# Cross attention's scores in two fp32r passes on split operands, with the pieces of the round laid out anew

## The reference

```python
q = _split_heads(query @ q_w + q_b, B)          # 16 heads of 16
k = _split_heads(key @ k_w + k_b, B)
v = _split_heads(value @ v_w + v_b, B)
scores = jnp.einsum('bhqd,bhkd->bhqk', q, k) * SCALE
attn = jax.nn.softmax(scores, axis=-1)
out = jnp.einsum('bhqk,bhkd->bhqd', attn, v)
return out.transpose(0, 2, 1, 3).reshape(B, -1, EMBED_DIM) @ o_w + o_b
...
x = _layernorm(x + _L0_xattn_ref(x, ctx_1024, ctx_1024, ...))
logits = x @ gate_w
w, sel = jax.lax.top_k(softmax(logits), 2)      # two of eight experts, beside two shared ones
```

## Time and profile before

| | |
|---|---|
| median of 3 runs | 971.75 us (963.71 to 973.4) |
| the profiled execution | 971.51 us, span 969.7 us |
| PE matmul busy | 863.9 us, 89% of the span |
| PE weight loads | 648.7 us, 67% |
| DVE | 607.3 us, 63% |
| ACT | 451.7 us, 47% |
| POOL | 344.7 us, 36% |
| chain that ended last | PE 56%, DVE 15%, ACT 10%, DMA 6%, POOL 5% |

### The profile page before, as it was taken

How to read it: one execution, slowest core, us unless ns; L and a number is a source line. 1 busy time by engine, 2 the same in 40 slices (tenths; PEclk the granted TensorE clock), 3 DMA queues, 4 the chain that set the end, 5 groups by cost and what they waited for, 6 DMA issues and landing times.

```text
span 969.7 us, 18401 instructions
## 1 busy us (share of the span) xinstructions
PE 863.9 (89%) x6886; PEld 648.7 (67%) x6886; DVE 607.3 (63%) x1410; ACT 451.7 (47%) x845; POOL 344.7 (36%) x336
## 2 busy tenths in 40 slices
PE   8897789779999986998899889989997999999994
PEld 6665566667777765786566556556785777777774
DVE  6998697576889988533567786774462343333255
ACT  5777555446666655442244534445331323222221
POOL 8422200123557566312001352233540242222684
PEclk9999899798999987999799999999999999999998
DMA  6799669897655432124991112002202222221421
GB/s 196 206 281 286 164 157 252 294 222 183 123 120 122 77 76 65 46 87 160 388 353 42 63 64 89 18 23 98 78 23 85 65 66 66 58 65 50 152 66 65
DMA packets 144468, 123.52 MB, mean 127 GB/s; under 512 B 89790, under 2 KB 126590, under 8 KB 143102
## 3 DMA queue, kind: packets, MB, share of 16 engines
q1 hardware_dynamic: 140974, 112.98, 41.8%
q0 software_dynamic: 3408, 9.38, 2.6%
HBM read 74.04 MB, written 48.29 MB: 126 GB/s over the span
## 4 chain that ended last, share of the span: by engine, by line
PE 56%; DVE 15%; ACT 10%; DMA 6%; POOL 5%; SPq 4%; issue 4%; POOLq 0%; DVEq 0%; ACTq 0%
PE ps L2527 10%; PE ps L1933 5%; PE ps L2542 5%; DVE cross_room L1966 3%; PE ps L2391 3%; PE ps L1873 3%; PE ps L1366 3%; PE ps L681 3%; PE ps L1634 3%; PE ps L437 2%; PE ps L1995 2%; POOL kept L2674 2%; PE ps L2404 2%; DMA hank<-rt_dram 2%; PE ps L1518 2%
## 5 line engine op out<-in xcount | busy, mean ns | idle before, releaser
L2011 ACT ACTIVATE cross_room<-ps 128x1024 f32<-128x1024 f32 x64 | 65.5, 1023 | 98.5 <-PE ps L1937 98.5
L2527 PE MATMUL ps<-wr,xbT 128*128 x312 | 99.0, 460 | 2.0 <-ACT xbT L2563 2.0
L1966 DVE TENSOR_REDUCE cross_room<-ps 128x4 f32<-128x1024 f32 x64 | 78.0, 1223 | 35.8 <-PE ps L1933 35.0
L1933 PE MATMUL ps<-kept,cross_room 32*128 32x256 f32 x512 | 74.5, 413 | 20.0 <-DVE cross_room L1966 18.4
L2616 POOL DMA_INDIRECT y_dram<-yb,dest_row x39 | 37.4, 960 | 133.4 <-DVE dest_row L2592 129.2
L1334 POOL TENSOR_TENSOR st<-st,exponent 128x20 f32<-128x20 f32 x16 | 56.8, 3548 | 62.4 <-DVE st L1309 61.1
L2527 PEld LDWEIGHTS ps<-wr,xbT 128*128 128x128 f32 x312 | 58.8, 189 | 29.6 <-issue 2.7
L1937 PE MATMUL ps<-cross_room,kept 32*128 32x256 f32 x512 | 75.6, 414 | 0.0
L1933 PEld LDWEIGHTS ps<-kept,cross_room 32*128 32x128 f32 x512 | 47.3, 191 | 37.9 <-issue 18.4
L565 DVE SCALAR_TENSOR_TENSOR room<-room 128x256 f32<-128x256 f32 x144 | 58.3, 479 | 9.7 <-ACT room L514 9.7
L2601 DVE TENSOR_TENSOR cross_room<-cross_room,ps 128x352 f32<-128x352 f32 x39 | 20.3, 521 | 58.8 <-PE ps L2527 58.8
(11 more groups left out here) (355 smaller groups left out, 2234.5 us busy)
## 6 DMA issues: line engine op xcount, KB each, us to landing
xs_dram<-params SPq DMA_DIRECT2D x17, 1040.0 KB, 17.9
room<-in_gW SPq DMA_DIRECT2D x8, 1280.0 KB, 8.9
tok_dram<-room SPq DMA_DIRECT2D x8, 768.0 KB, 6.7
fir_dram<-room SPq DMA_DIRECT2D x6, 1024.0 KB, 7.3
paths<-fir_dram SPq DMA_DIRECT2D x48, 128.0 KB, 3.7
xb<-xs_dram SPq DMA_DIRECT2D x39, 130.0 KB, 2.4
hank<-rt_dram SPq DMA_DIRECT2D x8, 512.0 KB, 8.4
yr<-y_dram SPq DMA_DIRECT2D x16, 256.0 KB, 3.1
```

What stands on the lines that cost most here:

```text
L1933: m1 = nc.tensor.matmul(ps[:, c, t * T:(t + 1) * T], strips(qS[b % 3], g, c)[:, t * P:(t + 1) * P], kS(b, g)[c * CH:(c + 1) * CH], start=T ...
L1966: V.tensor_reduce(mx[:, :, g, XD + 2 * h * CH:XD + (2 * h + 1) * CH + 1:CH].rearrange("p t c -> p c t"), ps[:, pair(h), :].rearrange("p c ...
L2011: S.activation(pT[g % 2][:, pair(h)].rearrange("p c k t -> p (c k t)"), ps[:, pair(h), :].rearrange("p c n -> p (c n)"), ACT.Exp).then_inc ...
L2527: m = nc.tensor.matmul(ps[:, 2 * (j % 2) + half, 0:FF], xbT[j % 2][:, k, :], wr[:, bass.ds(e, 1), k, half, :].rearrange("p e n -> p (e n)" ...
```

## The change

- **Scores in two fp32r passes.** fp32 operands q and k become pieces: `qA` (the query rounded to fp32r by ACT from PSUM, with the bias), `qB` (what is left, by DVE from PSUM: `scalar_tensor_tensor`, to which the maxima are added as before), `kA` and `kB` for the keys. The 16 rows of a strip that were free hold the head's dimensions a second time (the weights are copied into both halves, and the biases loaded into both), so that two passes over 32 rows (kA with qA, kB with qB) give the sum of all the products. A slot has 16 PE records as before, 8 fp32 matmuls before and 16 fp32r now.
- **Keys split by POOL.** `pool_keys(b, half)`: three POOL instructions for half a batch, six a batch, a round ahead; batch 0 at the phase's start, ahead of the blanks' memset.
- **The query in four pieces** instead of two halves; ACT evicts qA (two instructions a half), DVE forms qB in slots 4 and 7.
- **Router logits** come straight out of PE with tokens on the partitions (L2113): no 8x256 product, no copy by ACT, no turning back.
- **o_b** is added to the residual by POOL before it is needed, not by DVE after; the layer norm's scale and shift goes from DVE to ACT, for which POOL makes -mean*rstd (four small instructions instead of two).
- **Laid on other rounds or slots:** the maxima's turning of half 0 from slot 5 to 6; the router's index work, its weights and the placing; the shared expert's casts (round 5, slots 1 and 4) and subtractions (round 6, slots 1 and 5); the routed weights of experts 3 to 7 are loaded after the last scores (`sp_last`), since kA and qB stand in their room.
- **Before the phase:** 16 instead of 8 bias DMAs, eight instead of four copies of weights by POOL, no bias additions and no memsets of these weights, three small DVE instructions for masks.

```diff
+        def pool_keys(b, half):
+            pool.wait_ge(s.p2_made, SLOTS * (b - 2))
+            k, high = env.kS_half(b, half), halves(kA[b % 3], half)
+            pool.in_turn()
+            G.tensor_scalar(high, k, env.upper, 0.0, ALU.mult, ALU.add).then_inc(*pool.tick(s.keys))
+            pool.in_turn()
+            G.tensor_tensor(high, k, high, ALU.subtract).then_inc(*pool.tick(s.keys))
+            pool.in_turn()
+            G.tensor_scalar(env.x2T[half][:, :, b * T:(b + 1) * T], k, env.lower, env.max_row, ALU.mult,
+                            ALU.add).then_inc(*pool.tick(s.keys))
...
         def act_queries(b):
...
             for half in range(2):
+                act.wait_ge(s.q_made, XG * b + 2 * half + 2)
+                for g in range(2 * half, 2 * half + 2):
+                    m = S.activation(qA[b % 3][:, g, :], queries(b, g), ACT.Identity, bias=bq[:, g:g + 1])
+                m.then_inc(*s.q_evicted.up())
+                yield
+                yield
+                yield
...
         def dve_queries(b):
...
-                dve.wait_ge(s.q_made, 2 * b + half + 1)
-                for g in range(2):
-                    m = V.tensor_scalar(qS[b % 3][:, 2 * half + g, :], bank(f"q{half}", b)[:, g * T:(g + 1) * T],
-                                        bq[:, 2 * half + g:2 * half + g + 1], None, ALU.add)
+                dve.wait_ge(s.q_evicted, 2 * b + half + 1)
+                for g in range(2 * half, 2 * half + 2):
+                    m = V.scalar_tensor_tensor(out=qB[b % 3][:, g, :], in0=queries(b, g), scalar=bq[:, g:g + 1], in1=qA[b % 3][:, g, :],
+                                               op0=ALU.add, op1=ALU.subtract)
...
         def pe_scores(b, slot):
...
             for t in range(TT):
-                if b < B:
-                    for c in range(2 * h, 2 * h + 2):
-                        m1 = nc.tensor.matmul(ps[:, c, t * T:(t + 1) * T], strips(qS[b % 3], g, c)[:, t * P:(t + 1) * P],
-                                              kS(b, g)[c * CH:(c + 1) * CH], start=True, stop=True)
...
+                for part, q in enumerate((qA, qB)):
+                    if b < B:
+                        for c in range(2 * h, 2 * h + 2):
+                            k = strips(kA[b % 3], g, c) if part == 0 else kB(b, g)[c * CH:(c + 1) * CH]
+                            m1 = nc.tensor.matmul(ps[:, c, t * T:(t + 1) * T], strips(q[b % 3], g, c)[:, t * P:(t + 1) * P], k,
+                                                  start=(part == 0), stop=(part == 1))
...
         def act_output(b):
...
+            act.wait_ge(s.rstd, 4 * b + 4)
+            for t in range(TT):
+                S.activation(y[b % 2][:, t, 0:D], y[b % 2][:, t, 0:D], ACT.Identity, bias=mv[:, t, 0:1],
+                             scale=mv[:, t, 1:2]).then_inc(*s.applied.up())
```

235 lines of the change are left out of this document (138 added, 97 removed).

## The result

The changed kernel takes 976.96 us (median of 20 runs, 971.18 to 986.54), the kernel before 971.62 us beside it (20 runs, 963.71 to 982.41): ratio 1.0069, 95% interval 1.0047 to 1.0091. The forecast was 949 us, faster. Beside the experiments the unedited changed kernel was timed and profiled twice more, on two chips: 968.59 us, ratio 1.0034 (0.9987 to 1.0081), and 965.91 us, ratio 0.9957 (0.9925 to 0.999). Which chip gave the first result is not on record. All three are within 1%: the change moved the time by next to nothing where 2.3% were expected.

A forecast was written before the change was run, and what follows sets the result against it. PE's work was taken to bound the round: 20.5 us plus 2.8 of waits gives 23.3 against 25.82. Over the rounds 203.2 became 180.6, 22.6 less with 0.5 given back, so 971.5 gives 949 us (939 to 959).

The forecast's parts named there:

- slot of scores: Cross attention's score matmuls: a slot falls from 1.08 to 0.70 us if four fp32r strips run together, 3.0 a round.
- PE's work, full round: Cross attention: PE's work falls from 23.8 to about 20.5 us by scores (3.0) and router logits (0.2).
- waits: slot 4, slot 6, slot 7: PE waits of the new order: 0.9 us for q's bank, 1.0 for PV's copy, 0.5 for the last exponential.
- Rival A: Score slot does not shrink because weight loads keep fp32r groups 0.2 us apart; about 966 us; chance 0.12.
- the rule of the Trainium skill: Scores: a weight load overlaps matmuls in flight only if its row group differs, so the slot stays near 1.08 us.
- rival C: POOL becomes the bound: from 1.8 us per key multiplication the kernel is slower, at 2.5 it takes 991 us; chance 0.10.
- Rival B: DVE and POOL hold each other up, stretching short DVE instructions beyond 0.5 us; 963 us; chance 0.13.
- the one of slot 0 to 1: Start of a round: PE has 1.0 us of turnings against a gap of 1.36 + 0.1, so waits 0.4.
- POOL's keys are ready before the first query is: Cross attention's start: POOL's key split, 3 us for a half, was costed as ready before the first query.
- I let that cost stay: Round 2: part of its time was at the lower clock (granted 0.81); that cost was kept in its 24 us.
- The prediction's own warning: Phases before or behind cross attention moving by over 3 us would mean something costed at nothing was not hidden.
- 0.5 of a possible 3.7: Before cross attention: eight more bias DMAs put SP back 3.7 us; later loads come 0 to 3.7 late, 0.5 taken.

The follow-up runs named there:

- the pair of profiles with filling: Idle transposes put in TensorE's two gaps behind cross attention, in the changed kernel (966.42 us, ratio 0.9999) and in the best kernel (948.55 us, 0.9768).
- the wait, the split and the weights moved: Changed kernel, DVE's wait for POOL's tables moved to first use, POOL's shared-expert subtractions to round 8, first weights three steps later: 952.8 us, ratio 0.984.
- the best kernel: Changed kernel with DVE's tables wait, POOL's shared-expert subtractions, first weights and bias loads moved: 954.27 us, ratio 0.9818; with idle transposes 948.55 us, ratio 0.9768.

## Why the prediction was wrong

The sum, step by step, against the two undisturbed profiles of the changed kernel. Its rounds 3 to 8 in the third one:

```profile
495.66:518.70 23.04, 20.55 (x257) 14.22 (x254) 15.23 (x23) 13.99 (x20) 9.09 (x14) 1.00 0.74 263
518.70:541.84 23.14, 20.99 (x262) 14.64 (x258) 18.45 (x45) 14.08 (x21) 10.56 (x15) 1.00 0.04 13
541.84:564.97 23.13, 20.97 (x260) 14.64 (x256) 18.58 (x45) 16.14 (x24) 14.69 (x19) 1.00 0.11 37
564.97:592.48 27.51, 23.75 (x261) 16.33 (x257) 19.01 (x45) 14.14 (x21) 20.96 (x23) 0.88 0.11 35
592.48:616.88 24.40, 22.32 (x262) 15.90 (x258) 19.16 (x45) 14.07 (x21) 13.34 (x18) 0.92 0.05 18
616.88:637.86 20.98, 17.89 (x240) 12.19 (x236) 16.12 (x41) 12.03 (x16) 7.78 (x12) 1.00 0.07 26
```

| step | forecast | measured |
|---|---|---|
| slot of scores | 0.70 | 0.67 |
| PE's work, full round | 20.5 | 21.0 |
| waits: slot 4, slot 6, slot 7 | 0.9, 1.0, 0.5 | 0.98, 0.54, 0.45 |
| multiplication of the keys | 0.8 | 0.69 and 0.77 |
| rounds 3, 4, 5, 8 | 22.8, 23.3, 23.7, 21 | 23.0, 23.1, 23.1, 21.0 |
| round 2 | 24 | 20.8 |
| round 6, round 7 | 25.5, 23.3 | 27.5, 24.4 (25.2, 23.1 at full clock) |
| round 9, to the shared expert | 18.7 | 22.1 (20.8 with one fall less) |
| start and round 1 | 18.9 | 29.2 |
| before the phase | 0.5 more | 2.5 to 6 more |
| shared expert and rest | 0 | 8 more |

**Right:** what the main argument rested on. Strips with fp32r weights run together as those in fp32 do. Rival A, and the rule of the Trainium skill, "TensorE: Matmul & The Clock Gate" (Part 3, "The mechanism"), as I put it, are refuted by the 0.67 us; the page's own sentence also lets a load go ahead through the background weight buffer, which I had left out. PE's many waits for DVE's reduce (18.4 us in all) are down to 3.1 us in four, and the waits that took their place are the ones named. From the lists of PE's waits over cross attention and the shared expert (total us, times, longest), before and then changed (third profile):

```profile
PE ps L1933 <- DVE cross_room L1966: 18.4, 23, 3.5
```

```profile
PE ps L2055 <- ACT coT L2066: 8.0, 7, 2.7
PE ps L2210 <- DVE qB L1935: 3.9, 4, 1.0
PE ps L1997 <- DVE cross_room L2026: 2.5, 2, 2.1
PE ps L1986 <- DVE cross_room L2026: 0.6, 2, 0.4
```

The keys' multiplications take 0.69 and 0.77 us, where rival C needed 1.8, and POOL is far from its bound (10.6 us of round 4, 14.7 of round 5, where 16.8 was laid out) but for round 6 with its subtraction (21.0). Rival B asked for more than two short DVE instructions a round over 0.5 us: there are at most two a round, the longest of these two profiles 0.94 us (in the first profile one took 2.88, in round 6, as in the kernel before).

That a full round came out at 23.1 for 23.3 is in part luck: PE's work was put 0.5 us too low and the waits 0.65 too high (2.15 measured of 2.8, the one of slot 0 to 1 is not there at all). In rival A's sum the waits should be 2.0 by its own terms, not 1.9; nothing hangs on it.

**Wrong, the start.** "POOL's keys are ready before the first query is" was true (453.6) and answered the wrong question. The keys were put in front of POOL's tables, and DVE's program waits for the tables before its first query of this phase (the kernel before has the same wait, with no keys ahead of the tables). I named what POOL must have ready and not who stands queued behind what it does later. 4.6 us of the start went with the wait, and 4.2 more since TensorE, idle for it, did round 1 at the lower clock. Of the remaining 1.8 us, 0.3 are the second step from qA to qB: with the bias loads spread the start takes 5.38 us, against 5.04 before, and the projection of q 3.72 in both. The other 1.4 are the clock again, since in the kernel with the wait moved the same projection took 5.13. "Round 1 unchanged" fell with it.

**Wrong, the clock.** "I let that cost stay" took the clock as fixed to its place in the kernel before. It does not stay in its place: of the 10 us at the lower clock in the old round 2 about 5 are left (granted 0.87 for 0.81), and the round gained 3.2 us on its forecast; others came in round 1, in rounds 6 and 7 (3 us, behind the wait of 2.7, though in one of four profiles with that wait they stayed away), in round 9 and behind cross attention. Most stand behind a gap of TensorE; that a gap alone decides is not shown. Their sum is what turned the result: about 4 + 3 + 1 + 7.5 lost, 3 gained.

**Wrong, the phases behind.** Of the 8 us, the late weights are excluded as far as the kernel before can tell. 1 us is the longer wait for the last scale and shift (2.53 for 1.48: moved to ACT, they stand behind its cast and behind a fourth POOL instruction). Two falls worth 3 us stand behind gaps, the one behind this wait and the one behind the gap of 2.2 us that the kernel before has too, and both went in the pair of profiles with filling. The rest is the clock too, by the busy times above, but what brought it down is not shown. The prediction's own warning (over 3 us means that something costed at nothing was not hidden) pointed here.

**Mis-sized, round 9.** The prediction gives its 17 in the table without a working. With no next batch behind it, the round is a chain with waits: 1.82 us for the copy of PV's output, 0.45 for the exponential, 0.75 at the end, 3.0 in all, and it takes 22.1 us where 18.7 was forecast. At least 1.3 of these 3.4 us are the clock once more: in the kernel with the tables' wait moved the same three waits stand in a round 9 of 20.8 us, with one fall where the changed kernel has two.

```profile
635.03:655.81 20.78, 17.51 (x180) 12.65 (x177) 6.62 (x34) 12.60 (x17) 9.00 (x13) 0.94 0.13 36
```

**Mis-sized, the phase before.** The 8 loads were put at 0.5 of a possible 3.7; the profiles say nearer the upper end (about 4 us in the kernel before with the loads), the times cannot tell.

Against cross attention's forecast of 201.2: start and round 1 +10.2, round 2 -3.2, rounds 3 to 5 and 8 -0.5, rounds 6 and 7 +3.1, round 9 +3.4, sum 214.2; measured 214.2 and 214.4. In the profile that belongs to the result the late signals add 6.7. With 8 behind and 2.5 to 6 before, all of the 22 us are given back.

With the wait, the split and the weights moved, the same scores give 952.8 us, and 948.55 with the bias loads spread and two gaps filled, about the time that was forecast, but by other steps than the forecast's (cross attention takes 199.2 us there, and the code behind it still 4.1 us more than before). The gain in the rounds was there, and was lost at the ends of the phase and to the clock.

## What to carry to other kernels

Where a piece is put in front of others on an engine, ask what that engine owed to whom behind it, and look for waits that stand in a program as a barrier ahead of their first use. A saving inside rounds can be lost where TensorE's idle gaps elsewhere grow: one wait of 3.3 to 6.3 us at the phase's start (4.83 in the first profile) stood ahead of a round 1 at the lower clock in every profile that had it, and cost 4.2 us in clock beside 4.6 in waiting. A forecast from one profile should say for each stretch which clock it had and whether the gaps that set it stay.

## What the runs showed of the hardware

- Two fp32r passes on four 32-row strips: 0.67 us for 16 records of 256 columns, against 1.08 us for the fp32 ones; in both, the four records of a group, one on each strip, start within 0.02 us of each other.
- The granted clock fell to the lower level after gaps of TensorE of 2.2 and 2.5 us. It did not always: a wait of 2.5 us was followed by no fall in one of nine profiles that had it, one of 2.65 us in round 6 in one of four, and the same 2.2 us gap in the kernel before left the clock alone in three profiles of four. With idle transposes in the gaps both falls vanished in the best kernel. The Trainium skill, "TensorE: Matmul & The Clock Gate" ("HAM oscillation — how this bites in real kernels"), describes the clock falling in waits; the gaps here are shorter than those it describes.
- Identical code (the routed experts) took 232.9 us without and 236.1 us with two more falls of the clock of 3.4 us each.
- TensorE's signals landed up to 2.5 us after their matmuls in one of three profiles of the same kernel, beside POOL's indirect DMAs; 6.7 us. The cause is open.
